# Graph attention on one core: inverse roots on GpSimd instead of ScalarE and VectorE, the last queries amid the first scores, the last weights cast in parts

## The reference, cut to what matters

```python
h = relu(layernorm(x))                                   # x [2048, 256]
hs = layer_norm(h, ln1) ; ht = layer_norm(h_target, ln1) # both with a rsqrt(var + 1e-5) per row
q = (ht @ Wq + bq) / sqrt(32) ; k = hs @ Wk + bk ; v = hs @ Wv + bv      # 8 heads of 32
logits = where(adj != 0, q k^T, -1e30) ; probs = softmax(logits)         # per head 2048 x 2048
ht = layer_norm(ht + (probs v) @ Wo + bo, ln2)
out = x + ht + gelu(ht @ W1) @ W2
```

## Time and profile before

| | |
|---|---|
| runs shown, median (lowest to highest), us | 494.72 (494.25 to 494.77) |
| the profiled execution, its own time, us | 494.16 |
| its span, first to last instruction, us | 492.5 |
| mean granted clock of PE over the span | 0.995 |
| PE busy | 473.9 us, 96% |
| DVE busy | 419.1 us, 85% |
| ACT busy | 377.1 us, 77% |
| POOL busy | 305.4 us, 62% |

### The profile page before, as it was taken

The page is one execution under the profiler, slowest core; times in us unless marked ns, Lnnn a source line. Parts: engine busy times, 40 slices in busy tenths (PEclk is TensorE's granted clock), DMA queues, the critical chain, the costliest instruction groups (busy, mean ns, idle before and its releaser), DMA issues.

```text
span 492.5 us, 10622 instructions
## 1 busy us (share of the span) xinstructions
PE 473.9 (96%) x4366; PEld 244.3 (50%) x4366; DVE 419.1 (85%) x631; ACT 377.1 (77%) x456; POOL 305.4 (62%) x152
## 2 busy tenths in 40 slices
PE   3999979999999999999999999999999999999995
PEld 1567523433333333333333333343434888888884
DVE  6889479999999999999999999999997977666343
ACT  4987968998998898998898998999995570727150
POOL 1000019996998999999999998999998300000000
PEclk9999989999999999999999999999999999999999
DMA  8997789723543674222772400070000100202021
GB/s 232 266 219 124 186 249 402 236 44 63 200 74 44 67 171 79 44 46 46 82 179 50 83 2 3 12 207 1 2 2 1 46 28 17 87 1 85 1 85 45
DMA packets 53774, 46.92 MB, mean 95 GB/s; under 512 B 35486, under 2 KB 46652, under 8 KB 53212
## 3 DMA queue, kind: packets, MB, share of 16 engines
q1 hardware_dynamic: 51216, 37.30, 28.3%
q0 software_dynamic: 2480, 8.92, 10.7%
q10 hardware_dynamic: 28, 0.01, 0.0%
HBM read 31.93 MB, written 14.81 MB: 95 GB/s over the span
## 4 chain that ended last, share of the span: by engine, by line
PE 61%; DVE 14%; issue 13%; ACT 5%; POOL 5%; DMA 1%; DVEq 0%; POOLq 0%
PE acc L1421 14%; PE slot L1406 13%; DVE probs L1032 10%; PE acc L1439 6%; PE slot L1521 3%; PE slot L1520 3%; PE slot L1519 3%; POOL added_up L547 3%; PE acc L1557 2%; PE acc L1558 2%; PE acc L1556 2%; PE slot L1472 2%; PE slot L1308 2%; DVE stats L852 1%; PE slot L1328 1%
## 5 line engine op out<-in xcount | busy, mean ns | idle before, releaser
L1032 DVE SCALAR_TENSOR_TENSOR probs<-maskT,slot 128x1024 f32<-128x1024 uint16 x256 | 298.4, 1217 | 8.1 <-PE slot L1406 7.8
L753 ACT ACTIVATE probs<-probs 128x1024 f32<-128x1024 f32 x256 | 267.0, 1057 | 25.7 <-DVE probs L1032 7.2
L547 POOL TENSOR_TENSOR added_up<-added_up,probs 128x1024 f32<-128x1024 f32 x96 | 226.7, 2417 | 1.0 <-ACT probs L753 0.9
L1421 PE MATMUL acc<-probs,V 128*32 128x512 f32 x1024 | 137.1, 607 | 1.0 <-ACT probs L753 1.0
L1439 PE MATMUL acc<-probs,ones 128*32 128x256 f32 x1024 | 77.1, 379 | 0.0
L1439 PEld LDWEIGHTS acc<-probs,ones 128*32 128x32 f32 x1024 | 33.3, 110 | 72.8 <-issue 71.2
L1406 PE MATMUL slot<-q_hi,k_hi 32*128 32x512 f32 x512 | 64.8, 496 | 3.8 <-DVE probs L1032 3.5
L544 POOL TENSOR_TENSOR added_up<-probs 128x1024 f32<-128x1024 f32 x16 | 38.1, 2411 | 29.4 <-ACT probs L753 18.8
L1406 PEld LDWEIGHTS slot<-q_hi,k_hi 32*128 32x128 f32 x512 | 24.6, 182 | 61.9 <-DVE probs L1032 55.2
L810 ACT ACTIVATE g_full<-slot 128x512 f32<-128x512 f32 x32 | 19.3, 602 | 45.2 <-issue 30.0
L1406 PE MATMUL slot<-q_lo,k_hi 32*128 32x512 f32 x512 | 52.0, 392 | 0.0
(11 more groups left out here) (142 smaller groups left out, 496.7 us busy)
## 6 DMA issues: line engine op xcount, KB each, us to landing
adj_raw<-in_adj POOLq DMA_DIRECT2D x16, 512.0 KB, 5.4
htn<-in_L_gnn_h_target SPq DMA_DIRECT2D x4, 512.0 KB, 5.7
ht_saved<-htn SPq DMA_DIRECT2D x1, 2048.0 KB, 6.8
k_hi_saved<-k_hi SPq DMA_DIRECT2D x1, 2048.0 KB, 10.6
k_lo_saved<-k_lo SPq DMA_DIRECT2D x1, 2048.0 KB, 14.1
v_saved<-V SPq DMA_DIRECT2D x1, 2048.0 KB, 9.0
inverse<-inverse_saved SPq DMA_DIRECT2D x8, 256.0 KB
maskT<-in_L_gnn_W SPq DMA_DIRECT2D x2, 1024.0 KB, 12.3
```

The costliest lines, as they stand in the source:

```text
L547: nc.gpsimd.tensor_tensor(added_up[:, pair], added_up[:, pair], at(i), ALU.add).then_inc(added, 1)
L753: nc.scalar.activation(p, p, ACT.Exp).then_inc(exped, 1)
L1032: nc.vector.scalar_tensor_tensor(out=probs[:, u % RING], in0=m, scalar=-HALF_EDGE, in1=slot[u % SLOTS][:], op0=ALU.add, op1=ALU.min).then_ ...
L1421: mm = pe.matmul(acc[HD * j:HD * j + HD, 0, :], V[:, i, h * HD:(h + 1) * HD], probs[:, (PAIRS * k + j // 2) % RING, j % 2, :], start=(i == 0),
```

## The change

Three parts.

1. The inverse roots of the first stage. POOL makes each with one operation, `spread` to the power of -0.5 (`tensor_tensor` with a tile of -0.5, `ALU.pow`), on 128x2 elements for the halves of chunk 0 and 128x4 for the others. ACT's `Sqrt` and DVE's reciprocal and Newton step go. ACT's warm-up function is `Exp` instead of `Sqrt`. POOL makes one such power on ones ahead of all, with its result unused. The power operations stand in POOL's queue between the loads of adj.
2. The queries of target chunk 3. Their projection goes to `acc` instead of a slot, one group behind `scores(0)`, the other behind `scores(1)`; ACT makes their high parts ahead of exponentials 0 and 2, DVE their low parts ahead of masks 2 and 4, and the first weighing, which writes `acc`, waits for all of them. The queries of chunks 1 and 2 swap their slots. SP stores the queries in the order 2, 0, 1, 3.
3. The casts of W1 and W2. Four parts each, after exponentials 210, 215, 220, 225 and 230, 235, 240, 245. SP issues the loads of W1 and W2 ahead of spreading the inverses of chunk 2 instead of behind.

```diff
@@ first stage, POOL @@
+            nc.gpsimd.memset(minus_half[:], -0.5).then_inc(halves_made, 1)
+            def root_of(r, w, tiles, signal):
+                nc.gpsimd.tensor_tensor(r, w, minus_half[:, 0:tiles, :], ALU.pow).then_inc(signal, 1)
...
+            pool.wait_ge(halves_made, 1)
+            root_of(newton[:], ones[:, 0:TILES][:, :, None], TILES, halves_made)
+            root_half(0)
+            root_half(1)
             pool.wait_ge(x_in[2], 16)
             load_adj(0, 0)
             pool.wait_ge(x_in[3], 16)
             load_adj(0, 1)
+            source_root(1)
+            source_root(2)
             load_adj(0, 2)
+            source_root(3)
             load_adj(0, 3)
+            target_root(0)
+            target_root(1)
             load_adj(1, 0)
+            target_root(2)
+            target_root(3)
             load_adj(1, 1)
@@ ACT: its root_of, root_half, source_root, target_root and their calls go @@
-            nc.scalar.activation(warm[:], ones[:, 0:1], ACT.Sqrt).then_inc(warmed, 1)
+            nc.scalar.activation(warm[:], ones[:, 0:1], ACT.Exp).then_inc(warmed, 1)
@@ DVE: inverse_root goes @@
             def scale_rows(ts, into0, base, tiles):
-                inverse_root(spread[:, ts, :], rstd[:, ts, :], norm_h, base, tiles)
                 nc.vector.tensor_tensor(rstd[:, ts, :], rstd[:, ts, :], nodes[:, ts][:, :, None], ALU.mult
                                         ).then_inc(norm_h, 1)
@@ queries @@
+        PROJECTED = (acc, slot[1], slot[2], acc)
...
             for u in range(PAIRS * NT):                  # ACT
+                if u in (0, 2):
+                    queries_hi(LAST, [u // 2])
                 exponentials(u)
...
             for u in range(PAIRS * NT):                  # DVE
+                if u in (2, 4):
+                    queries_lo(LAST, [u // 2 - 1])
                 mask(u)
...
             def queries(c, groups=range(GROUPS)):        # PE
                 if c == 0:
                     pe.wait_ge(q_scaled, 2)
                 elif c == 1:
+                    pe.wait_ge(k_lo_out, GROUPS * NCH)
+                elif c == 2:
                     pe.wait_ge(v_out, NCH)
-                elif c == 2:
-                    pe.wait_ge(k_lo_out, GROUPS * NCH)
                 else:
-                    pe.wait_ge(q_lo_out, GROUPS * (c - 1))
+                    pe.wait_ge(q_lo_out, GROUPS)
...
                 if k == 0:                               # scores
                     pe.wait_ge(t_affine, DC * NCH)
-                    pe.wait_ge(q_lo_out, GROUPS * LAST)
+                    pe.wait_ge(q_lo_out, GROUPS * 2)
                     pe.wait_ge(k_lo_out, GROUPS * NCH)
                 elif k == 1:
-                    pe.wait_ge(q_lo_out, GROUPS * NCH)
+                    pe.wait_ge(q_lo_out, GROUPS * LAST)
                     pe.wait_ge(masked, 1)
...
                 if k == 0:                               # weigh
-                    pe.wait_ge(v_out, NCH)
+                    pe.wait_ge(q_lo_out, GROUPS * NCH)
...
             scores(0)
+            queries(LAST, [0])
             scores(1)
+            queries(LAST, [1])
@@ casts, ACT @@
-                    nc.scalar.copy(w1_hi[:], w1_raw).then_inc(w1_hi_made, 1)
-                    nc.scalar.copy(w2_hi[:], w2_raw).then_inc(w2_hi_made, 1)
+                if step < SPLITS:
+                    d, fs = step // 2, slice(step % 2 * FF // 2, (step % 2 + 1) * FF // 2)
+                    nc.scalar.copy(w1_hi[:, d, fs], w1_raw[:, d, fs]).then_inc(w1_hi_made, 1)
+                elif step < 2 * SPLITS:
+                    fs = slice((step - SPLITS) * FC // SPLITS, (step - SPLITS + 1) * FC // SPLITS)
+                    nc.scalar.copy(w2_hi[:, fs, :], w2_raw[:, fs, :]).then_inc(w2_hi_made, 1)
@@ SP @@
-            for c in (2, 3, 0, 1):
+            for c in (2, 0, 1, 3):
                 keep_queries(c)
...
                     if c < LAST:
                         turn_mask(c + 1, 0)
+                    else:
+                        sp.wait_ge(masked, UC * c)
+                        sp.dma_start(w1_raw, W1.rearrange("(c p) n -> p c n", p=P)).then_inc(w1_in, 16)
+                        sp.dma_start(w2_raw, W2.rearrange("(f p) n -> p f n", p=P)).then_inc(w2_in, 16)
                     spread_inverse(c - 1)
```

More of the change, by code:

```diff
@@ L622, in rectify_chunk @@
                 rectify(range(c * TILES, (c + 1) * TILES))
[L624 to L637, removed]
-                                     ).then_inc(rooted_t, 1)
             def normalise(ts):
@@ L783, in _ @@
                     evacuate_sums(u // UG - 1)
[L784 to L785 removed]
+                if u >= SPLIT_FROM and (u - SPLIT_FROM) % SPLIT_EVERY == 0:
+                    split_weights((u - SPLIT_FROM) // SPLIT_EVERY)
             evacuate_context(NCH * GROUPS - 1)
@@ L856, in row_stats @@
                 dve.wait_ge(signal, done + 2 * tiles)
-            def inverse_root(w, r, signal, done, tiles=TILES):
-                step = newton[:, 0:tiles, :]
-                nc.vector.reciprocal(r, r).then_inc(signal, 1)
-                dve.wait_ge(signal, done + 1)
-                nc.vector.tensor_tensor(step, r, r, ALU.mult).then_inc(signal, 1)
-                dve.wait_ge(signal, done + 2)
-                nc.vector.scalar_tensor_tensor(out=step, in0=w, scalar=-0.5, in1=step, op0=ALU.mult,
-                                               op1=ALU.mult).then_inc(signal, 1)
-                dve.wait_ge(signal, done + 3)
-                nc.vector.scalar_tensor_tensor(out=r, in0=step, scalar=1.5, in1=r, op0=ALU.add, op1=ALU.mult
-                                               ).then_inc(signal, 1)
-                dve.wait_ge(signal, done + 4)
             def centre_rows(ts, done, tiles):
@@ L951, in keys_lo, with queries_lo @@
                                                    op0=ALU.add, op1=ALU.subtract).then_inc(k_lo_out, 1)
-            def queries_lo(c):
+            def queries_lo(c, groups=range(GROUPS)):
                 hi, lo = queries_made(c)
-                for g in range(GROUPS):
+                for g in groups:
                     dve.wait_ge(q_hi_out, GROUPS * c + g + 1)
-                    nc.vector.scalar_tensor_tensor(out=lo[:, g, :], in0=(acc if c == 0 else slot[1 + c % 2])[:, g, :],
+                    nc.vector.scalar_tensor_tensor(out=lo[:, g, :], in0=PROJECTED[c][:, g, :],
                                                    scalar=qbias[:, g:g + 1], in1=hi[:, g, :].bitcast(F32),
@@ L1301, in turn_target, with project @@
                 turn(acc if c == 0 else slot[0], htn, c * TILES, t_turned, normed_t)
-            def project(dst, w, hT, signal, ready, c):
-                for g in range(GROUPS):
+            def project(dst, w, hT, signal, ready, c, groups=range(GROUPS)):
+                for g in groups:
                     for d in range(DC):
@@ L1331, in values, with queries @@
                     mm.then_inc(v_projected, 1)
-            def queries(c):
+            def queries(c, groups=range(GROUPS)):
                 if c == 0:
@@ L1386, in _ @@
             queries(2)
-            queries(3)
             def scores(k):
```

61 lines of the change are left out of this document (29 added, 32 removed).

## The result

The changed kernel takes 499.23 us (median of 5 runs, 497.0 to 500.34) against 494.77 us (5 runs, 494.25 to 495.41) of the kernel before on the same chip: ratio 1.0079, 95% interval 1.005 to 1.0109. It is slower by 0.5 to 1.1%, where 489.9 was forecast and 492.8 was the upper end of the range. The interval is made without runs over 1.5% above the kernel's fastest; a kernel whose own times are spread as widely as that loses part of its upper runs by it, so for such kernels I give the runs themselves.

What follows compares the result with a forecast made beforehand. PE and DVE were both taken as full in the middle stage (76 to 366 us), so its start, PE's waits and what follows bind. 3.6 + 0.3 + 1.0 - 0.1 = 4.8 us gave 489.9, range 488.9 to 492.8.

Steps and rivals of the forecast that it cites:

- The loads wait for transposes anyway: POOL's queue, first stage: roots of chunks 1 and 2 delay a load of adj some 0.5 us, at cost 0.
- the load of 37.78: POOL's queue: nearest load that could hold up a root, 0.53 us long, its first target root ready only after 39.
- d = 1.0: d is the time of one power on POOL, taken as 0.7 us; at 1.0 part 1 would win 0.
- (a): Rival, first-stage roots: slow power, kernel slower from d = 2.1 on, 496.1 us at d = 2.4; chance 0.12.
- (b): Rival, first-stage roots: power between 1.2 and 2.1 us, 0.2 to 4 gained, 492.5 in the middle; chance 0.13.
- 3.6 predicted: Part 2, last queries amid the scores: fifth scores 3.9 us earlier at 72.9, of which 0.3 is part 1's.
- start at 69.4: Part 2, PE's walk: first weighing runs 69.4 to 70.4, once DVE's last low half is done.
- 4.2 - 1.4 + 0.9: Part 2 on DVE: first mask 4.2 us earlier, two low parts take 1.4 back, half-clock waits return 0.9.
- part 1's 0.3: First-stage inverse roots on POOL: chunk 2 normalised earlier, 0.3 us kept to the scores.
- Rival (c): Start of the middle stage: clock falls to 0.50 behind PE's waits between 67.5 and 72.9, giving 491.3 us; chance 0.17.
- 0.87 for 0.9: Part 3, casts in eight parts: two PE waits of 0.50 go, 1.0 us, less 0.1 for late weights.
- rival (d): Last group: cast parts don't help, copies make PE wait or weights land late, giving 490.9 us; chance 0.13.

Runs made afterwards that it cites:

- the queue, and the quick pace: The changed kernel plus a 16-byte transfer issued by POOL directly ahead of each load of adj rows 2 to 5: 493.32 us, ratio 0.9961.
- the roots first: The changed kernel with POOL's list reordered so no root stands behind a load waiting for a transpose: 488.74 to 490.88 and 495.71 to 498.81 us, median 495.86.
- the near twin: The changed kernel with the tile of -0.5 at 64 bytes a partition instead of 16: 497.38 us, ratio 1.0012.
- the 16-byte transfers: One 16-byte POOL transfer directly ahead of each load of adj rows 2 to 5, added to the changed kernel with the roots first: 489.43 us, ratio 0.9889.
- part 1 put right: The changed kernel with POOL's roots moved ahead of waiting loads and the 16-byte transfers added: 489.43 us, ratio 0.9889.
- the kernel with parts 2 and 3: The changed kernel without part 1, roots made by ACT and DVE as before: 490.52 us, ratio 0.9927.
- only the source side on POOL: The changed kernel with the target side's roots put back on ACT and DVE: 491.04 us, ratio 0.9943.
- one early power: Parts 2 and 3 without part 1, plus a fill of -0.5 and one unused power at the head of POOL's list: 490.89 us, ratio 0.9931.

## Why the prediction was wrong

**The step that failed** stands in part 1, POOL's queue: "The loads wait for transposes anyway [...]: 0", and "A load that waits could hold up a root queued behind it; the nearest case is the load of 37.78", whose root is ready after 39. The mechanism was named, and then priced by the time of the old trace, as if the transposes would stay as they were. The load came at 42.22, behind a transpose of 16.5 us instead of 11.9, and the next one at 55.36, behind one of 13.1 instead of 7.5; the second was not priced at all. DVE lost 2.5 and 4.6 us to the two roots behind them, for a term put at nothing. Queue and pace feed each other: how long a load holds up the roots is how long a transpose takes. With neither the kernel takes 489.4; with the queue, and the quick pace in the traced run, 493.3; with the roots first and the slow pace in the traced run 488.7 to 498.8, most runs in the upper group; with both 499.2, or 492.2 to 500.55 in the near twin. What makes the transposes slow stays open. The prediction had no rival for it: all four turned on a slow power, the clock or the casts. Its sum, 489.9, is close to the 489.4 that the change gives with the roots first and the 16-byte transfers added. That is in part luck: of that version's 5.3 us part 1 has about 1 instead of 0.3, and part 2 has 3.4 instead of 3.6.

**The power** was taken as 0.7 us; it measured 0.70 on 128x2 and 1.00 to 1.04 on 128x4. Chunk 1's chain on DVE's timeline, as the earlier trace rows:

```profile
16.46 0.16 DVE L900 TENSOR_TENSOR spread<-spread,second 128x4 f32<-128x4 f32 x1
17.78 0.16 DVE L904 TENSOR_TENSOR rstd<-rstd,nodes 128x4 f32<-128x4 f32 x1 [1.15 <-POOL rstd L540]
17.98 0.16 DVE L907 SCALAR_TENSOR_TENSOR shift<-second,rstd 128x4 f32<-128x4 f32 x1
```

From 16.62 to 18.14, 1.52 us for the old 1.43, where 1.34 was expected. By the prediction's own terms d = 1.0 makes part 1 worth 0, and rivals (a) and (b) fall. Measured, part 1 put right is worth about 1 us (489.43 against 490.52; 4 runs each, on different chips, and their intervals, 0.9873 to 0.9906 and 0.9904 to 0.995, just touch), so its sign is probable and no more. Chunk 2 was normalised at 26.89, ahead of the 27.6 to 27.8 forecast; the lead over before was there ahead of this chain, whose spread was ready 1.15 us earlier than in the earlier trace rows (25.21 against 26.36).

**The code load.** The first power, the throwaway of 3.35, took 1.04 us like the later ones, and the root of the first half was done at 8.18. The Trainium skill, "GPSIMD Engine Reference", section "Instruction dispatch", lets the first call of newly loaded code pay about 6 us; no run here shows it for this operation.

**Part 2** was mis-sized: 3.6 predicted, 3.4 left in the time and 2.7 at the fifth scores. The walk let the first weighing start at 69.4; it starts at 70.8 in the kernel with parts 2 and 3, because ACT and DVE make the last query half later than walked. The prediction's own sum over DVE said so: 4.2 - 1.4 + 0.9 is 3.7 and not 3.9, and less part 1's 0.3 it is the 3.4 measured. In the kernel with parts 2 and 3 DVE has no idle time from 70 to 76 us and the clock stays at 1.00, as predicted.

**Rival (c)** did not fall. The clock did drop near 72 us in two of the traced kernels with parts 2 and 3: to 0.64 over 70 to 72 and 0.51 over 72 to 74 with only the source side on POOL, and to 0.62 over 72 to 74 and 0.53 over 74 to 76 with one early power. PE's timeline of the first:

```profile
70.50 1.93 PE L1441 MATMUL acc<-probs,V 128*32 128x512 f32 x8 [1.83 <-DVE q_lo_staged L977]
72.35 0.80 PE L1426 MATMUL slot<-q_hi,k_hi 32*128 32x512 f32 x4
```

These two traced runs took 491.35 and 491.48 us, near the 491.3 of the rival; five with parts 2 and 3 and no drop there took 489.99 to 490.56. The wait of PE was 1.83 us in this trace, and 1.82 both in the other one and in the trace of parts 2 and 3, where the clock stayed full, so the length of that wait does not decide by itself. In the changed kernel the drop at 58 to 64 us stands behind PE's wait for the held-up root.

**Part 3** was right: 0.87 for 0.9. W1 and W2, issued at 312.83 and 313.34 instead of from 309.4 on, landed 5.0 and 7.7 us after their issues, ahead of the first cast of 324.64; rival (d) fell.

## What to carry to other kernels

Work that someone waits for should not stand in an in-order queue behind a transfer that waits, and if it must, price it by what the transfer waits for in the new kernel, not by its time in the old trace: the transpose issued near 26 us took 11.9 us in one kernel here and 21.0 in another. Putting arithmetic between the DMA issues of an engine can change the pace of transfers that have nothing to do with it, so after such a move read the landing times of all transfers beside those issues. When a change of several parts loses, run it without the part that has the least to win: here that one experiment turned a loss of 0.8% into a gain of 0.7%. And a trace is one run: where the runs of a kernel are spread, look at their times before reading a cause out of it.

## What the runs showed of the hardware that was not expected

- A transpose by DMA (128 rows of adj, 512 KB) landed in 4.3 us alone (issued at 80.77 in the changed kernel), in 7.4 to 9.8 beside a load that POOL issued at the same moment, and in 12.7 to 13.3 beside the same load when its first packet came 0.72 to 0.84 us behind the transpose's instead of 0.42 to 0.57. The load beside it landed in 12.2 in the changed kernel instead of 5.9.
- PE's clock fell to 0.50 to 0.53 (1.2 GHz for most of the stretch) behind a wait of 1.82 or 1.83 us in two traces, and stayed at 1.00 (2.4 GHz) behind one of 1.82 in another.
- A load of adj took POOL 0.53 or 0.54 us to issue behind another load, 0.55 to 0.57 behind a 16-byte transfer, 0.57 behind an addition and 0.59 behind a power.
- A power on POOL is dear for its size but not out of reach: 0.70 us for 2 elements a partition, 1.00 to 1.04 for 4, against 0.20 for an addition of 4. From these two sizes I estimate about 0.4 us and 0.15 us an element.
- A kernel can have two times: with the roots first, about 489 or about 497 from one run to the next, on the same chip and code. A single profile of such a kernel shows one of them.
